# Cross attention in a decoder layer: the value matmuls of two units issued together over four column groups, and three steps of the loop moved

## What is computed

```
def _L0_xattn_ref(x, context, w_qkv, w_proj, b_proj):
    qkv = (x @ w_qkv.T).reshape(B, N, 3, H, D).transpose(2, 0, 3, 1, 4)
    q, k, v = (qkv[0], qkv[1], qkv[2])
    kv = context.reshape(B, N_c, 2, H, D).transpose(2, 0, 3, 1, 4)
    k = jnp.concatenate([kv[0], k], axis=2)
    v = jnp.concatenate([kv[1], v], axis=2)
    attn = softmax(jnp.einsum('bhnd,bhmd->bhnm', q * D ** -0.5, k))
    out = jnp.einsum('bhnm,bhmd->bhnd', attn, v)
    return out.transpose(0, 2, 1, 3).reshape(B, N, C) @ w_proj.T + b_proj
...
    logits = xf @ gate_w.T
    top_p, top_i = jax.lax.top_k(jax.nn.softmax(logits, axis=-1), K)
```

## Time and profile before

| | us |
|---|---|
| median of three runs | 1031.72 (1031.46 to 1033.61) |
| the profiled execution | 1039.75 |
| its span, first to last instruction | 1037.6 |
| PE, DVE, ACT, POOL busy in it | 890.1, 735.6, 583.9, 522.5 |

### The profile page before, as it was taken

One profiled execution on the slowest core, in us unless ns is written; L12 is line 12 of the kernel. 1 busy time (PEld: TensorE's weight loads), 2 busy tenths in 40 slices (PEclk: granted clock), 3 DMA queues, 4 the chain that ended last, 5 costly groups with the idle time before them and its releaser, 6 DMA issues.

```text
span 1037.6 us, 29477 instructions
## 1 busy us (share of the span) xinstructions
PE 890.1 (86%) x11511; PEld 709.6 (68%) x11511; DVE 735.6 (71%) x1859; ACT 583.9 (56%) x1367; POOL 522.5 (50%) x909
## 2 busy tenths in 40 slices
PE   4899999999999999689888888888888865988770
PEld 3688888888888888566666666666666644766560
DVE  4888888888888888567778778778778755433352
ACT  2577667767677776556666566666666533422220
POOL 4345544444444455334444754754754645465662
PEclk9899999999999999979999999999999975988995
DMA  9970000000000000000000100100104002222416
GB/s 208 159 193 2 2 2 2 2 2 2 2 2 2 2 3 2 11 12 12 12 12 13 32 23 13 34 25 15 33 19 132 25 18 78 72 74 78 127 35 176
DMA packets 54653, 43.31 MB, mean 42 GB/s; under 512 B 10163, under 2 KB 48362, under 8 KB 54516
## 3 DMA queue, kind: packets, MB, share of 16 engines
q1 hardware_dynamic: 49568, 32.97, 13.4%
q0 software_dynamic: 4608, 8.30, 2.5%
q10 hardware_dynamic: 340, 0.14, 0.1%
HBM read 21.46 MB, written 21.12 MB: 41 GB/s over the span
## 4 chain that ended last, share of the span: by engine, by line
PE 60%; DVE 23%; issue 8%; ACT 3%; DMA 2%; another core or an unknown queue 2%; POOL 1%; SPq 0%; DVEq 0%; POOLq 0%; ACTq 0%
PE ps L1170 50%; DVE nmax L1037 10%; PE ps L1221 7%; DVE kT L937 2%; DVE q_part L937 2%; DMA w_qkv<-in_L_attn_W_v 1%; DVE bst L1063 1%; DVE padded L1081 1%; DMA raw_gu<-y_part 1%; DVE bst L1056 1%; DVE zT L1029 1%; ACT xT_hi L727 1%; DVE padded L1078 1%; PE ps L1502 1%
## 5 line engine op out<-in xcount | busy, mean ns | idle before, releaser
L1037 DVE TENSOR_REDUCE nmax<-ps 128x2 f32<-128x512 f32 x256 | 163.9, 683 | 37.4 <-PE ps L1170 36.5
L734 ACT ACTIVATE probsT<-ps 128x512 f32<-128x512 f32 x256 | 139.5, 601 | 59.8 <-PE ps L1170 57.7
L661 ACT ACTIVATE probs<-ps,nmax 128x128 f32<-128x128 f32 x512 | 142.9, 382 | 10.8 <-DVE nmax L801 10.5
L1170 PE MATMUL ps<-probsT,va 128*32 128x128 f32 x2048 | 138.9, 278 | 5.2 <-ACT zT L739 4.8
L495 POOL TENSOR_TENSOR probs<-probs,rinv 128x512 f32<-128x512 f32 x128 | 133.0, 1039 | 18.8 <-DVE rinv L811 18.8
L655 ACT COPY probsT<-ps 128x512 f32<-128x512 f32 x128 | 75.1, 587 | 87.3 <-PE ps L1221 87.2
L1170 PEld LDWEIGHTS ps<-probsT,va 128*32 128x32 f32 x2048 | 104.7, 111 | 23.6 <-issue 16.6
L801 DVE TENSOR_REDUCE nmax<-ps 128x4 f32<-128x512 f32 x128 | 83.5, 673 | 38.0 <-PE ps L1170 38.0
L626 POOL DMA_INDIRECT y_part<-wo_all,slot_ids x80 | 78.2, 977 | 59.5 <-DVE wo_all L1128 36.4
L1170 PE MATMUL ps<-xT_hi,w 128*128 128x128 f16 x1024 | 98.7, 222 | 5.8 <-DVE raw_gu L845 3.8
L1170 PE MATMUL ps<-xT_lo,w 128*128 128x128 f16 x512 | 91.3, 222 | 0.0
(11 more groups left out here) (224 smaller groups left out, 2190.7 us busy)
## 6 DMA issues: line engine op xcount, KB each, us to landing
slots<-blank SPq DMA_DIRECT2D x1, 5200.0 KB, 43.3
w<-slots SPq DMA_DIRECT2D x16, 325.0 KB
y_part<-blank SPq DMA_DIRECT2D x2, 2048.0 KB, 31.8
ctx_row<-in_ctx SPq DMA_DIRECT2D x32, 128.0 KB
raw_gu<-y_part SPq DMA_DIRECT2D x16, 256.0 KB
out_x<-x_all SPq DMA_DIRECT2D x8, 256.0 KB, 4.1
y_part<-wo_all,slot_ids POOLq DMA_INDIRECT x80
slots<-rows,slot POOLq DMA_INDIRECT x64
```

Of the source, the lines that this page charges most:

```text
L661: last = nc.scalar.activation(probs[:, u, i * P:(i + 1) * P], ps[u][:, i * P:(i + 1) * P], ACT.Exp, bias=nmax[:, u, i:i + 1])
L734: last = nc.scalar.activation(probsT[:, 2 * (t % 2) + a, :], ps[2 + a][:, :], ACT.Exp)
L1037: last = nc.vector.reduce_max(nmax2[:, b % 2, t:t + 2, l + a], ps[a][:, :].rearrange("p (t k) -> p t k", t=2), AX_X, negate=True)
L1170: return nc.tensor.matmul(o, l, r, start=start, stop=stop, **kw)
```

## The change

1. `apply_values(n, pair)` takes two units at once: 16 matmuls, in which four neighbours go to four column groups. Units 0 and 1 are applied in the third step behind the transposed scores; units 2 and 3 in the first step of the next round, behind the query projection and ahead of the shift. The exponentials of units 2 and 3 go to the tile `probs`. Whoever counted four applications a batch counts two.
2. The matmuls of the context's keys and ACT's copy of them (`kT`) move from the third step to the fourth, ahead of the value projection.
3. The transpose of the third norm's rows moves from the third step to the fourth, between that of the second norm's rows and that of z; DVE's copy of it takes the place that the copy of the logits had.
4. The logits matmul moves from the fourth step to the next round's first, behind the output projection; DVE copies the logits there between `q_part` and the residual sum. The router's first instruction waits for that copy.
5. In self-attention DVE normalises the next rows (`xn`) ahead of the two halves of the key copies, not behind them.

The diff, cut to its core:

```diff
@@ pool
                         if valid(-2):
-                            pool.wait_ge(ca_values_applied, UNITS * (b - 2) + UNITS)
+                            pool.wait_ge(ca_values_applied, 2 * (b - 2) + 2)
@@ act
-                    if g == 2 and valid(1):
+                    if g == 3 and valid(1):
                         n = b + 1
                         act.wait_ge(ca_keys_in_bank, n + 1)
...
                     if valid(-1):
-                        t = UNITS * (b - 1) + g
-                        act.wait_ge(ca_scores_T, t + 1)
-                        if t >= 2:
-                            act.wait_ge(ca_values_applied, t - 1)
+                        act.wait_ge(ca_scores_T, UNITS * (b - 1) + g + 1)
+                        if valid(-2):
+                            act.wait_ge(ca_values_applied, 2 * (b - 2) + g // 2 + 1)
                         for a in range(2):
-                            last = nc.scalar.activation(probsT[:, 2 * (t % 2) + a, :], ps[2 + a][:, :], ACT.Exp)
+                            last = nc.scalar.activation(exp_cells[g][a], ps[2 + a][:, :], ACT.Exp)
@@ dve
+                    if g == 1 and valid(2):
+                        n = b + 2
+                        dve.wait_ge(sa_rstd, n + 1)
+                        nc.vector.tensor_scalar(xn[:, :], x_all[:, n, :], mv[:, 0, 0:1], rstd[:, 0:1],
+                                                ALU.subtract, ALU.mult).then_inc(sa_norm, 1)
...
-                    if g == 2 and valid(-3):
-                        nc.vector.tensor_copy(xT3[:, :], ps[7][:, 2 * P:3 * P]).then_inc(ff_xT_taken, 1)
...
                         if valid(-3):
-                            nc.vector.tensor_copy(logits[:, b - 3, :], ps[7][:, 3 * P:3 * P + NE]).then_inc(logits_taken, 1)
+                            nc.vector.tensor_copy(xT3[:, :], ps[7][:, 2 * P:3 * P]).then_inc(ff_xT_taken, 1)
...
+                    if g == 0 and valid(-4):
+                        dve.wait_ge(logits_in_bank, b - 3)
+                        nc.vector.tensor_copy(logits[:, b - 4, :], ps[7][:, 3 * P:3 * P + NE]).then_inc(logits_taken, 1)
@@ pe
-            def apply_values(n, u):
-                pe.wait_ge(ca_exp, UNITS * n + u + 1)
+            def apply_values(n, pair):
+                pe.wait_ge(ca_exp, UNITS * n + 2 * pair + 2)
...
-                for t in (2 * (u // 2), 2 * (u // 2) + 1):
+                for t in (2 * pair, 2 * pair + 1):
                     for k in range(2):
-                        for a in range(2):
-                            l = 2 * (u % 2) + a
+                        for l in range(4):
                             last = mm(ps[4][ROWS * l:ROWS * l + ROWS, t * P:(t + 1) * P], va[:, n % 3, k, 4 * t + l, :],
-                                      probsT[:, buf + a, (2 * (t % 2) + k) * P:(2 * (t % 2) + k + 1) * P],
+                                      exp_cells[2 * pair + l // 2][l % 2][:, (2 * (t % 2) + k) * P:(2 * (t % 2) + k + 1) * P],
...
+                    if g == 0 and valid(-2):
+                        apply_values(b - 2, 1)
                     if g == 0 and valid(-1):
                         pe.wait_ge(ca_max_padded, b)
...
-                    if g == 0 and valid(-2):
-                        apply_values(b - 2, UNITS - 1)
                     if valid(-1):
                         transposed_scores(b - 1, g)
-                        if g > 0:
-                            apply_values(b - 1, g - 1)
+                        if g == 2:
+                            apply_values(b - 1, 0)
```

More of the change, by code:

```diff
@@ L279, in build @@
         y_in = raw_gu
+        exp_cells = [[(probsT, probs)[u // 2][:, 2 * (u % 2) + a, :] for a in range(2)] for u in range(UNITS)]
         bv_wide = probsT[:, 0:2, :].rearrange("p a q -> p (a q)")
@@ L949, in shift @@
                 own = slice(b0, b0 + n)
+                dve.wait_ge(logits_taken, b0 + n)
                 then(nc.vector.reduce_max(rt_a[:, 0:n], logits[:, own, :], AX_X))
@@ L1290, in prepare_cross @@
                 last.then_inc(bv_wo_summed, 1)
-            def apply_values(n, u):
-                pe.wait_ge(ca_exp, UNITS * n + u + 1)
-                if u == 0:
+            def apply_values(n, pair):
+                pe.wait_ge(ca_exp, UNITS * n + 2 * pair + 2)
+                if pair == 0:
                     pe.wait_ge(ca_context_values, n + 1)
@@ L1393, in cross_attention @@
                         last.then_inc(ca_shift_in_bank, 1)
[L1394 to L1397, removed]
+                    if g == 0 and (valid(-3) or valid(-4)):
                         for t, b0, r in routed(b - 1, 2):
@@ L1401, in cross_attention @@
                             pe.wait_ge(ca_xT_taken, n + 1)
-                        mm(ps[7][:, P:2 * P], zT2[:, :], wprojT[:, :]).then_inc(ca_output, 1)
+                        if valid(-4):
+                            pe.wait_ge(ff_xT_taken, b - 3)
+                        if valid(-3):
+                            pe.wait_ge(ca_zT_taken, b - 2)
+                            mm(ps[7][:, P:2 * P], zT2[:, :], wprojT[:, :]).then_inc(ca_output, 1)
+                        if valid(-4):
+                            mm(ps[7][:, 3 * P:3 * P + NE], xT3[:, :], gateT[:, :]).then_inc(logits_in_bank, 1)
                     if g == 1 and valid(1):
@@ L1428, in cross_attention @@
                         last.then_inc(ca_keys_in_bank, 1)
-                    if g == 2 and valid(-3):
-                        pe.wait_ge(ff_norm, b - 2)
-                        pe.wait_ge(ca_residual, b - 2)
-                        nc.tensor.transpose(ps[7][:, 2 * P:3 * P], xn3[:, :], ident[:, :]).then_inc(ff_xT_in_bank, 1)
                     if g == 3 and valid(1):
@@ L1442, in cross_attention @@
                         if valid(-3):
-                            pe.wait_ge(ff_xT_taken, b - 2)
+                            pe.wait_ge(ca_residual, b - 2)
+                        if valid(-4):
+                            pe.wait_ge(logits_taken, b - 3)
                         for t, b0, r in routed(b, 2):
@@ L1453, in cross_attention @@
                         if valid(-3):
-                            mm(ps[7][:, 3 * P:3 * P + NE], xT3[:, :], gateT[:, :]).then_inc(logits_in_bank, 1)
+                            pe.wait_ge(ff_norm, b - 2)
+                            nc.tensor.transpose(ps[7][:, 2 * P:3 * P], xn3[:, :], ident[:, :]).then_inc(ff_xT_in_bank, 1)
                         if valid(-2):
```

15 lines of the change are left out of this document (5 added, 10 removed).

## The result

The changed kernel takes 1058.31 us (median of four runs, 1054.46 to 1061.24) beside 1031.59 of the kernel before: 1.0257 times as long, interval 1.0215 to 1.0299.

The account below looks back on a forecast made before the run. Bound: PE in self-attention, a chain through several engines in cross attention (12.06 us a round). Sum: 1031.7 - 5.5 (loop) + 18 (half-clock stretches) = 1044 us; range 1024 to 1062.

Parts of the forecast that it names:

- The bound and the new chain: Cross-attention loop: a chain of waits through several engines sets a plain round, going from 12.06 to 11.65 us.
- Four column groups: Value matmuls on PE: four groups run at once, so a call of 32 instructions still takes 1.00 us.
- the third rival: Value calls in cross attention: four column groups do not run at once, total 1050 to 1080 us; chance 0.13.
- The idle piece: PE idles 1.8 to 2.2 us in nearly one piece ahead of the third scores in every cross-attention round.
- The falls: PE clock drops from 1.00 to 0.50 behind the idling in cross attention: 20 times at 0.9 us, +18 us.
- two in three: Share of long PE idle pieces followed by half clock, from three outside the loop; applied to some 30 rounds.
- The price: Cost of one clock drop to the chain's PE work in cross attention: 0.9 us, between 0 and 2.2.
- the wait for `padded`: PE waits ahead of the shift in cross attention; the value call placed there was said to cost nothing at 1.00 us.
- The scattering rounds: Twelve cross-attention rounds with scattering transfers, whose chain goes through POOL: +0.1 to +0.2 us each.
- Self-attention's norm: The norm moved on DVE in self-attention, beside a PE never idle: 0, at worst some tenths of a us.
- The page's rule: Skill page's limit on PE idle gaps, longer than the new piece; by it the idling in cross attention would be harmless.

Follow-up runs that it names:

- the keys moved alone: Kernel before, with only the context's keys matmuls and ACT's copy of them moved from the third step to the fourth; 0.9938 of the kernel before.
- the kernel filled in all rounds: Changed kernel plus eight unread 512-column matmuls behind z's transposes and, in scattering rounds, six of 384 columns ahead of the fourth step's transposes; 1.0041 of the kernel before.
- the two moves alone: Kernel before, with only the third norm's row transpose and copy, the logits, and self-attention's norm moved as in the change; 1.0064 of the kernel before.
- POOL's order: Changed kernel without the two-unit value calls, with POOL's scattering transfer of the second step moved behind the second norm; 0.9848 of the kernel before.
- the kernel filled with four: Changed kernel plus four unread 512-column matmuls on PE behind the transposes of z in the third step; 1.0034 of the kernel before.

## Why the prediction was wrong

**The bound and the new chain: right.** The sum of 11.65 us for a plain round was 11.67 in the kernels whose clock held; the seventeen rounds without scattering came out at -0.41 on average (-7.0 in sum), forecast -0.35. That the keys copy enters the chain while the packing leaves it is shown by the keys moved alone.

**Four column groups: right.** 32 instructions in 1.02 us; the third rival is out.

**The idle piece: right in place and nearly in size** (mostly 2.06 us, 2.41 in some rounds, forecast 1.8 to 2.2), and that the clock falls behind it.

**The falls: mis-sized, the first of the two steps that failed.** I took two in three of 30 rounds at 0.9 us, 18 us. There were 26. The 25 that begin in the 26 rounds make these 26.4 us longer than in the kernel filled in all rounds, 1.1 each; that is 8 us more in all, and most of it is the number. "Two in three" was the share among three pieces of other stages, too few for a rate, and not all that the trace has. Behind self-attention it holds four more of 1.8 us and above that begin at a clock of 1.00 with work to come:

```profile
442.04 0.58 PE L1170 MATMUL ps<-ident_h,keys 128*128 128x128 f16 x4 [2.60 <-DVE kT L937]
...
876.24 0.80 PE L1502 MATMUL ps<-ident_h,w 128*128 128x128 f16 x6 [3.42 <-DVE w_lo L1108]
...
938.95 0.48 PE L1170 MATMUL ps<-xg,w_hi 128*128 128x384 f16 x2 [2.24 <-issue]
...
982.04 0.80 PE L1170 MATMUL ps<-xg,w_hi 128*128 128x384 f16 x2 [3.01 <-issue]
...
441.90:455.50 13.60, 12.08 (x110) 8.02 (x112) 8.16 (x17) 6.25 (x12) 4.54 (x13) 0.50 0.04 11
834.40:841.20 6.80, 5.62 (x57) 3.84 (x53) 1.76 (x10) 2.65 (x5) 2.27 (x5) 0.50 0.01 2
875.40:882.20 6.80, 4.91 (x22) 2.74 (x23) 1.68 (x3) 3.01 (x7) 0.94 (x6) 0.50 0.37 125
940.30:947.00 6.70, 5.27 (x25) 4.20 (x26) 2.23 (x5) 2.16 (x4) 2.79 (x5) 0.50 0.25 74
981.20:988.00 6.80, 5.23 (x21) 2.87 (x22) 3.17 (x7) 1.98 (x5) 3.45 (x6) 0.50 0.08 24
```

In or behind each of the four the clock went to 0.50. So six of seven pieces came with a fall, not two of three, and six in seven of 30 rounds is 26, the number that came; that seven pieces of other stages meet it so well is in part luck. The stretch at 0.50 behind 832.98, too, is 6.8 us long (834.40 to 841.20), where my row had only its first 3.4.

The price was nearly right on average (1.1 against 0.9), but it is two prices. In the six rounds from 475.75 to 558.51 a fall that lasts 6.8 us costs 2.0 us a round (13.67 against 11.67), near the upper end of what I had allowed (2.2): 1.28 between the third scores and the keys, and 0.71 between the keys and the shift (4.73 from 503.14 to 507.87, 4.02 in the kernel filled in all rounds), where the value call, costed at nothing under the wait for `padded`, has no cover when PE is slow. The other falls cost some 0.8 each.

**The scattering rounds: mis-sized, the second step.** I took +0.1 to +0.2, with a gain of up to 0.2 because POOL's first transfer leaves earlier. They are +0.45 where no fall is in them, in the kernel filled in all rounds as with the two moves alone (+0.58 in the former with its one fall). The gain did not come: POOL stood waiting for DVE's statistics instead,

```profile
POOL ve L533 <- DVE mv L1064: 79.6, 25, 4.3
...
609.36 0.19 POOL L533 TENSOR_SCALAR ve<-mv 128x1 f32<-128x1 f32 x1 [3.25 <-DVE mv L1064]
```

(waits of the changed kernel, 470 to 800 us: total, times, longest; and one in a scattering round of the kernel filled in all rounds). The three additions to that chain, 0.21 + 0.12 + 0.07 = 0.40, then stood in full, and are within 0.05 of the 0.45; it was the upper end of my range (0 to +0.4), and I had chosen below the middle.

The two account for most of the gap of 14.4 us: 8 us or more are falls, and in twelve scattering rounds some 3.6 (0.45 instead of 0.15 each). The kernel filled in all rounds is 4.2 us slower than before (1.0041 of 1030.32), while its 26 rounds are 1.8 us shorter. Of these 6 us, 3 are in the round that follows the 26, one with scattering (15.32 us with a fall, 12.35 before), and 2.4 between the last keys run and the experts (64.8 us against 62.4). Setup and experts are not accounted for: there profiles differ by more than is missing. The experts and the output took 159.1 us in the kernel before's profile and 153.9 in the changed one's, which would also be most of the 8 us by which the former stands above its median.

**Self-attention's norm: right**, 1.0002.

**The page's rule against the trace.** By "TensorE: Matmul & The Clock Gate" of the Trainium skill ("Why this matters for your kernels") gaps as short as these should not bring the clock down. The runs decide against it, as the rows did: pieces of mostly 2.06 us, 26 falls.

## What to carry to other kernels

When matmuls get cheaper in a chain that another engine sets, the saved time turns into idling, and idling can cost the clock for what comes next. Ask where the saved microseconds will lie, and whether what stands behind them is in the chain. Here a few matmuls that nobody reads took back most of the loss (1.0257 to 1.0034), but only shortening the other engines' part made the kernel faster than before (the keys' place 0.9938, POOL's order 0.9848). A share ("two in three") should be counted over every such place of the trace, not over the few at hand. And an edit costed at nothing because of its cover needs the price without the cover as well, for the state in which the cover goes.

## What the runs showed of the hardware that I had not expected

The clock did not answer to the longest idle piece alone: 1.55 us in one place passed round after round (the kernel filled with four), and once 2.06 us in the changed kernel, while two pieces of 1.25 and 1.49 in a round were followed by a fall in some rounds (558.08) and not in others (533.00 and 538.56). And a POOL engine that only issues a scattering transfer is held for 0.97 to 1.09 us each time, so that the place of one of the four issues of a round was worth 1.5% of the kernel: 122.9 - 107.1 = 15.8 us in nine rounds, of which some 3 us are four falls that went with it.
